# Scores in smaller matmul tiles, fewer evictions, paced transfers and new engine orders in the last stage of a five-stage transformer kernel

## The reference, cut to what matters

```
for i in range(6):
    x = attn_layer(shift_tokens(x), Wqkv[i], q_scale[i], k_scale[i], Wo[i]) + x
    x = ffn_layer(shift_tokens(x), ln_g[i], ln_b[i], W1[i], b1[i], W2[i], b2[i]) + x
# attn_layer: 16 heads of 64
q = l2norm(q) * qs;  k = l2norm(k) * ksc
q = q * cos * scale + rotate_half(q) * sin * scale        # rotate_half: (-x2, x1)
k = k * cos / scale + rotate_half(k) * sin / scale
# local_attention: windows of 32 queries, each sees its own and the last window: 64 keys
sim = einsum('bhwie,bhwje->bhwij', bq, bk2) * 8.0
sim = where((it < jb) | (it > jb + 32) | (jb == -1), -max, sim)
out = einsum('bhwij,bhwje->bhwie', softmax(sim), bv2)
```

## Time and profile before

| | us |
|---|---|
| median of 3 runs | 4817.93 (4815.92 to 4821.29) |
| span of the profiled execution, first to last instruction | 4799.2 |
| TensorE busy in it | 4554.0 |
| VectorE busy | 3761.7 |
| GpSimd busy | 3692.6 |
| ScalarE busy | 3501.1 |

### The profile page before, as it was taken

The page is one execution under the profiler, slowest core; times in us unless marked ns, Lnnn a source line. Parts: engine busy times, 40 slices in busy tenths (PEclk is TensorE's granted clock), DMA queues, the critical chain, the costliest instruction groups (busy, mean ns, idle before and its releaser), DMA issues.

```text
span 4799.2 us, 114895 instructions
## 1 busy us (share of the span) xinstructions
PE 4554.0 (95%) x44512; PEld 3128.6 (65%) x44512; DVE 3761.7 (78%) x5226; ACT 3501.1 (73%) x6738; POOL 3692.6 (77%) x2336
## 2 busy tenths in 40 slices
PE   7998999987887799999999999999999999999997
PEld 5666768874443466666666666666666666666665
DVE  6776556658999688888888888888888888888885
ACT  3454756557775688888888888888888888888885
POOL 2222334438998999999999999999999999999993
PEclk9898999998999999999999999999999999999998
DMA  2000000004332222232222322232322322322222
GB/s 79 1 2 1 2 1 1 1 1 168 150 142 106 55 63 63 56 85 70 54 67 65 75 68 55 68 75 61 68 64 67 76 53 66 80 64 63 62 56 52
DMA packets 164292, 289.06 MB, mean 60 GB/s; under 512 B 44063, under 2 KB 61351, under 8 KB 159655
## 3 DMA queue, kind: packets, MB, share of 16 engines
q1 hardware_dynamic: 162310, 281.46, 22.3%
q10 hardware_dynamic: 1440, 0.24, 0.0%
HBM read 90.22 MB, written 2.62 MB: 19 GB/s over the span
## 4 chain that ended last, share of the span: by engine, by line
PE 59%; ACT 3%; issue 2%; DVE 1%; POOL 1%; ACTq 0%; DVEq 0%; POOLq 0%
PE ps L2559 18%; PE ps L2614 8%; PE ps L2588 8%; PE ps L2572 7%; PE ps L2627 7%; PE ps L2601 3%; PE ps L2669 3%; PE ps L2660 3%; PE ps L2653 3%; ACT L3f_pT L2820 2%; PE ps L2634 1%; PE ps L2640 1%; ACT L3f_kT L2803 1%; POOL L3f_t L3155 0%; POOL L3f_raw L3172 0%
## 5 line engine op out<-in xcount | busy, mean ns | idle before, releaser
L3155 POOL TENSOR_TENSOR L3f_t<-L3f_raw,L3f_rot 128x512 f32<-128x512 f32 x768 | 1007.7, 1334 | 268.3 <-DVE L3f_raw L2971 268.3
L2559 PE MATMUL ps<-L3f_wqkv,all_z 128*128 128x512 f32 x2304 | 1133.7, 601 | 12.8 <-DVE L3f_raw L2971 11.7
L3172 POOL TENSOR_TENSOR L3f_raw<-L3f_raw,L3f_t 128x1024 f32<-128x1024 f32 x384 | 961.4, 2504 | 3.8
L3164 POOL TENSOR_TENSOR L3f_raw<-L3f_raw,L3f_rot 128x1024 f32<-128x1024 f32 x384 | 953.8, 2484 | 3.8
L2971 DVE TENSOR_TENSOR L3f_raw<-ps,L3f_ri 128x512 f32<-128x512 f32 x768 | 495.6, 682 | 231.9 <-ACT L3f_ri L2778 230.2
L2954 DVE TENSOR_REDUCE L3f_ss<-L3f_sqr 128x8 f32<-128x512 f32 x768 | 507.8, 681 | 163.2 <-ACT L3f_sqr L2768 160.8
L2572 PEld LDWEIGHTS ps<-all_ident,L3f_raw 128*128 128x128 f32 x3072 | 358.7, 141 | 320.7 <-issue 282.8
L2559 PEld LDWEIGHTS ps<-L3f_wqkv,all_z 128*128 128x128 f32 x2304 | 385.2, 191 | 221.0 <-issue 151.5
L2572 PE MATMUL ps<-all_ident,L3f_raw 128*128 128x128 f32 x3072 | 472.3, 276 | 49.1 <-ACT L3f_kT L2803 27.1
L2820 ACT ACTIVATE L3f_pT<-ps 64x512 f32<-64x512 f32 x768 | 453.2, 590 | 83.9 <-PE ps L2601 75.9
L2768 ACT ACTIVATE L3f_sqr<-ps 128x512 f32<-128x512 f32 x768 | 449.9, 599 | 76.5 <-PE ps L2559 71.7
(11 more groups left out here) (333 smaller groups left out, 8702.0 us busy)
## 6 DMA issues: line engine op xcount, KB each, us to landing
L3f_vw<-L3f_v SPq DMA_DIRECT2D x1344, 128.0 KB, 2.4
L3a_Bs<-L3a_rows SPq DMA_DIRECT2D x16, 2048.0 KB, 7.1
L3a_Cs<-L3a_rows SPq DMA_DIRECT2D x16, 2048.0 KB, 11.6
L3f_vw<-L3f_v SPq DMA_DIRECT2D x192, 64.0 KB, 2.1
L3f_wqkv<-in_L_ffn_Wqkv SPq DMA_DIRECT2D x24, 256.0 KB, 2.9
L3f_wqkv<-in_L_ffn_Wqkv SPq DMA_DIRECT2D x6, 512.0 KB, 3.6
L3f_wo<-in_L_ffn_Wo SPq DMA_DIRECT2D x48, 64.0 KB, 2.3
out<-all_x SPq DMA_DIRECT2D x8, 256.0 KB, 3.6
```

Of the source, the lines that this page charges most:

```text
L2559: p.matmul(PS[:, j % 3, :], Z[:, u % NSEQ, t * P:t * P + P], w, start=True, stop=True).then_inc(proj.sem)
L3155: op = g.tensor_tensor(t[:, :, to], r[:, :, fr], w[:, 1, to].unsqueeze(1).broadcast_to((P, H, WIN)), ALU.mult)
L3164: g.tensor_tensor(r, r, w[:, 0, :].unsqueeze(1).broadcast_to((P, H, HD)), ALU.mult).then_inc(cosined.sem)
L3172: g.tensor_tensor(r, r, t, ALU.add).then_inc(rotated.sem)
```

## The change

It touches the last stage alone.

- Scores: q is evicted as it comes, into `qT`, in one operation for each group of four pairs; no zeros. A score matmul takes the 64 rows of one head, 32 columns of weights (a window's queries) and 64 keys. Windows go to the four quarters of the PSUM partitions, heads of a pair to banks 6 and 7. There are 64 matmuls a call in place of 32.
- The mask has one row of keys for all windows. `below` writes `sm` with the two heads of a pair side by side.
- `spread` evicts two blocks of 64 x 1024 in place of four of 64 x 512; `pT` still has its zeros, and the value matmuls keep their number and shape.
- `sine` is one operation, whose read goes through the halves of a head backwards.
- The 16 transfers of a unit have two semaphores in turn, and each waits for the last but one.
- The four lists of calls are in another order, and the outer loop runs from -4 to N/2 + 2.

```
-        lmaskb = self.sb("lmaskb", [P, TILES, 2, KEYS], BF16)
+        lmaskb = self.sb("lmaskb", [P, TILES, KEYS], BF16)
-        qz = self.sb("qz", [P, TILES, PAIRS, NW, 2, WIN])
+        qT = self.sb("qT", [P, TILES, PAIRS, P])
-        sm = self.sb("sm", [P, TILES, H, KEYS])
+        sm = self.sb("sm", [P, TILES, PAIRS, 2, KEYS])
-        pT = self.sb("pT", [P, TILES, 2 * PAIRS, 2, 2, WIN])
+        pT = self.sb("pT", [P, TILES, PAIRS, NW, 2, WIN])
 # sp
-                for part, shift in ((WIN, 0), (0, 1)):
-                    for half in range(2):
-                        for w in range(NW):
-                            ...
-                            s.dma_start(to, v2[...]).then_inc(v_put[k % 2].sem, 16)
+                pieces = [(part, shift, half, w) for part, shift in ((WIN, 0), (0, 1)) for half in range(2) for w in range(NW)]
+                for n, (part, shift, half, w) in enumerate(pieces):
+                    landed = v_put[k % 2][n % 2]
+                    if n >= 2:
+                        s.wait_ge(*landed.at(k // 2, 16 * (n // 2) - 1))
+                    ...
+                    s.dma_start(to, v2[w * WIN:(w + 1) * WIN, k % 2, 0:e, half, :]).then_inc(landed.sem, 16)
 # scores
-                        r = slice(w % 2 * HD, w % 2 * HD + HD)
-                        mm = p.matmul(PS[r, 6 + w // 2, a * KEYS:(a + 1) * KEYS], qz[:, t, a, w, :, :].rearrange("p h q -> p (h q)"),
-                                      kT[:, a, t * P + w * WIN:t * P + w * WIN + KEYS], start=True, stop=True)
+                        for h, (r, _) in enumerate(halves):
+                            mm = p.matmul(PS[w * WIN:(w + 1) * WIN, 6 + h, a * KEYS:(a + 1) * KEYS], qT[r, t, a, w * WIN:(w + 1) * WIN],
+                                          kT[r, a, t * P + w * WIN:t * P + w * WIN + KEYS], start=True, stop=True)
 # turned
-                    for half in range(2):
-                        r = slice(half * HD, half * HD + HD)
-                        op = a.activation(qz[r, t, 4 * g:4 * g + 4, :, half, :], src[r, :, :].rearrange("p c (w q) -> p c w q", q=WIN), ACT.Copy)
+                    op = a.activation(qT[:, t, 4 * g:4 * g + 4, :], src, ACT.Copy)
 # spread
-                for r in range(2):
-                    for half in range(2):
-                        op = a.activation(pT[half * HD:(half + 1) * HD, t, r:2 * PAIRS:2, :, half, :], ..., ACT.Copy)
+                for h, (r, _) in enumerate(halves):
+                    op = a.activation(pT[r, t, :, :, h, :].rearrange("p a w q -> p (a w) q"), PS[r, 4:6, :].rearrange("p b (n q) -> p (b n) q", q=WIN), ACT.Copy)
 # below
-                v.tensor_tensor(sm[:, t, :, :], sc(), mx[:, t, :].unsqueeze(2).broadcast_to((P, H, KEYS)), ALU.subtract).then_inc(s_sub.sem)
+                v.tensor_tensor(sm[:, t, :, :, :].rearrange("p a h k -> p h a k"), sc().rearrange("p (h a) k -> p h a k", h=2),
+                                mx[:, t, :].rearrange("p (h a) -> p h a", h=2).unsqueeze(3).broadcast_to((P, 2, PAIRS, KEYS)), ALU.subtract).then_inc(s_sub.sem)
 # sine
-                for half in range(2):
-                    to, fr = slice(half * WIN, (half + 1) * WIN), slice((1 - half) * WIN, (2 - half) * WIN)
-                    op = g.tensor_tensor(t[:, :, to], r[:, :, fr], w[:, 1, to].unsqueeze(1).broadcast_to((P, H, WIN)), ALU.mult)
-                op.then_inc(sined.sem)
+                g.tensor_tensor(t.rearrange("p h (b e) -> p h b e", b=2), r.rearrange("p h (b e) -> p h b e", b=2)[:, :, ::-1, :],
+                                w[:, 1, :].rearrange("p (b e) -> p b e", b=2).unsqueeze(1).broadcast_to((P, H, 2, HD // 2)), ALU.mult).then_inc(sined.sem)
 # outer loop
-        for i in range(-2, N // 2 + 1):
+        for i in range(-4, N // 2 + 3):
```

More of the change, by code:

```diff
@@ L2608, in values @@
                 if t == 0:
[L2609 removed]
+                    for e in range(2):
+                        p.wait_ge(*v_put[u % 2][e].all(u // 2))
                 for c in range(PAIRS // 2):
                     for w in range(NW):
[L2612 to L2616 removed]
+                        for to, n in halves:
+                            a = 2 * c + n
+                            mm = p.matmul(PS[to, 4 + c // 2, (c % 2) * 2 * P + w * HD:(c % 2) * 2 * P + (w + 1) * HD], vw[:, u % 2, t * NW + w, a * HD:(a + 1) * HD],
+                                          pT[:, t, a, w, :, :].rearrange("p h q -> p (h q)"), start=True, stop=True)
                 mm.then_inc(o_mm.sem)
@@ L2785, in value @@
                 if u >= 2:
-                    a.wait_ge(*v_put[u % 2].all(u // 2 - 1))
+                    for e in range(2):
+                        a.wait_ge(*v_put[u % 2][e].all(u // 2 - 1))
                 a.activation(v2[:, u % 2, int(x[1]), "ab".index(x[2]), :], PS[:, j % 3, :], ACT.Copy).then_inc(v_out.sem)
@@ L2872, in gelu @@
                     a.preload_act_table_set(EXP_LN)
-            value(2 * i + 2, "v1a")
+            affine(2 * i - 2)
+            exponent(2 * i, 1)
+            length(2 * i + 2, "q0")
+            turned(2 * i + 1, 0, 1)
+            turned(2 * i + 1, 0, 2)
+            squared(2 * i + 2, "k0a")
+            centred(2 * i - 1)
+            turned(2 * i + 1, 0, 3)
+            squared(2 * i + 2, "k0b")
+            root(2 * i - 1)
+            turned(2 * i + 1, 1, 0)
+            length(2 * i + 2, "k0")
+            value(2 * i + 2, "v0a")
+            turned(2 * i + 1, 1, 1)
+            spread(2 * i, 0)
+            value(2 * i + 2, "v0b")
+            squared(2 * i + 2, "q1a")
+            squared(2 * i + 2, "q1b")
+            turned(2 * i + 1, 1, 2)
+            output(2 * i, 0)
+            length(2 * i + 2, "q1")
+            turned(2 * i + 1, 1, 3)
+            squared(2 * i + 2, "k1a")
+            spread(2 * i, 1)
+            exponent(2 * i + 1, 0)
+            squared(2 * i + 2, "k1b")
+            affine(2 * i - 1)
+            exponent(2 * i + 1, 1)
+            output(2 * i, 1)
             gelu(2 * i - 1, 0)
             gelu(2 * i - 1, 1)
+            length(2 * i + 2, "k1")
+            value(2 * i + 2, "v1a")
             gelu(2 * i - 1, 2)
@@ L3172, in add @@
                 g.tensor_tensor(r, r, t, ALU.add).then_inc(rotated.sem)
+            add(2 * i + 2, "q0")
+            cosine(2 * i + 2, "k0")
+            add(2 * i + 2, "k0")
+            sine(2 * i + 2, "q1")
             cosine(2 * i + 2, "q1")
```

182 lines of the change are left out of this document (71 added, 111 removed).

## The result

The changed kernel takes 4793.8 us (median), the one before 4813.7 on the same chips: a ratio of 0.9967 with a 95% interval of 0.9952 to 0.9982. Faster by 0.3%, 16 to 20 us; the forecast was 170 us. Nearly all of the expected gain is missing, and the profile after shows three places where it went.

The account below looks back on a forecast made before the run. TensorE was taken to bound the last stage: 65.94 - 3.72 = 62.2 us a period, -175 us over 47 periods, +5 for layer changes, so 4817.9 - 170 = 4648 us. This case's range was 4570 to 4710, the overall range 4560 to 4815.

Parts of the forecast that it names:

- What bounds the kernel: Last stage: TensorE, busy 65.28 of 65.94 us a period; time saved there counts until GpSimd's 60.02 us stands in the way.
- lie beside TensorE: VectorE's mask, subtraction, sum and scaling: claimed unchanged, hidden beside TensorE with 11 us a period to spare.
- If all eight run beside each other it is 16 rounds of 59 ns = 0.94 us: Score call: 128 records in eight overlapping tiles; with 0.13 us kept beyond the rounds, 1.07 to 1.09 us.
- rival 1: Score matmuls: TensorE takes small records no faster than 28 to 29.5 ns, 3.6 to 3.8 us a call; about 5160 us, chance 0.17.
- rival 2: Score matmuls: no more than four tiles, or rows and columns not together; call stays 1.9 us; 4785 to 4820 us, chance 0.11.
- columns over tiles: Score matmuls: cost follows moving columns divided by tiles running side by side; 128 columns in one tile take 108 ns.
- 0.93 us a call: Score calls: time the new tiles were to save on TensorE, 3.7 us a period of four calls.
- TensorE's pieces are the same but for the scores: TensorE's work in the new orders: only scores change, each instruction waits only for data or banks; busy 61.6 of 62.2 us.
- The orders. I count 0, between -1.5 and +1.5: New lists of calls in the last stage: no effect counted, range -1.5 us (waits vanish) to +1.5 us a period.
- rival 3: GpSimd's reversed read costs more or new orders hold up the normalised rows; period 64 to 65 us, 4755 us, chance 0.16.
- The transfers: The values' 16 transfers, two at a time: train of about 20 us instead of 10.3, hidden before the values' matmuls.
- +5 us: Layer changes: weights queued behind the slower transfers stall TensorE 0 to 3 us, taken as 1 us in each of 5.

Follow-up runs that it names:

- e9: Changed kernel with ScalarE's three gelu calls together and q and k evicted as bfloat16, 128 instructions a score call: 0.9659 of the kernel before.
- e7: Changed kernel with the gelus together, score matmuls multiplying only 32 of 64 keys (output wrong): one run, 4776 us.
- e1: Changed kernel with ScalarE's three gelu calls next to each other again, the length of k1 behind them: 0.9905 of the kernel before.
- e8: Changed kernel with the gelus together and the other order of score tiles, heads outside and windows inside: 0.9897 of the kernel before.
- e6: Kernel before with score matmuls cut into 128 x 32 tiles, 256 instructions a call in place of 128: 1.0094 of the kernel before.
- e10: Kernel before with the new lists of calls and outer loop alone, gelus together: 1.0013 of the kernel before.
- e4: Changed kernel with the values' transfers issued back to back, as before: 1.0001 of the kernel before.
- e11: Changed kernel with the gelus together and the values' transfers back to back: 0.9913 of the kernel before.
- e14: Kernel before, with its old large score tiles, and q and k as bfloat16: 0.9797 of the kernel before.
- e2: Score tiles of the change alone, with the old lists of calls, back-to-back transfers and two sine operations: 0.9948 of the kernel before.
- e12: Repeat of e1 (changed kernel, gelus together) on the chip of e9 and e11: 0.9911 of the kernel before.
- e13: As e9, with every score matmul issued twice into the same place, 256 instructions a call: 0.9876 of the kernel before.

## Why the prediction was wrong

- **What bounds the kernel**: right as far as it went. TensorE had 65.28 of 65.94 us and the shortest period did follow the score call. VectorE's operations "lie beside TensorE" did not hold: their busy time stayed (3758 for 3762 us), but the longest waits of TensorE after, beside the standstills, are for VectorE.
- **"If all eight run beside each other it is 16 rounds of 59 ns = 0.94 us"** is the step that failed first. The eight do overlap, so rivals 1 and 2 are out. But between "columns over tiles" and rival 1's 28 ns lies a pace that I had only from a burst of eight: records are taken at 7.7 ns (e9, 0.485 us for 63 steps) to 8.6 (e7) at best and at 9.9 with f32 and 64 columns. The term "0.93 us a call" measured 0.61, 1.3 us a period less. My sign for this, 128 records in over 1.5 us, was too coarse: they took 1.48. The mean over 127 starts is 9.9 ns. By that, the 25 ns between starts that the Trainium skill states (TensorE: Matmul & The Clock Gate, section "Wait — 56ns, not 53.3ns?") does not hold across tiles.
- **"TensorE's pieces are the same but for the scores"** left out what the pieces are made of. The number of instructions per call doubled, from 128 to 256, and I priced their multiplying but not their arrival. Its price is 1.2 to 1.3 us a period on the mean (after, e1, e8), 1.0 in e6, where only the scores' instructions changed; the pauses at the borders alone sum to 49 us in the stage's 48 periods after.
- **"The orders. I count 0, between -1.5 and +1.5"**: the value was wrong and the cause could be read in the diff. `length` between two `gelu` calls means table loads; the trace of before had them at two lines, only around the trio. They cost 0.7 to 0.8 us a period (e1, e10). No rival of mine had the loads; rival 3 came nearest, since it had the new orders hold up the normalised rows, which is the way that the delay takes (`length`, `norm`, residual, `centre`; lines above). Its sum of 4755 us missed as well.
- **ScalarE**: 48 us a period forecast; e9 has 47.8 in 62.5. **GpSimd**: the one sine was to save 1.4 us a period. Its line's total fell from 1007.7 to 999.5 us in the run, about 0.2 a period: the mean is 2603 ns, the median 2367. I read the difference as longer operations that meet VectorE's scaling more often, which no run isolates. The reversed read itself costs nothing: the shortest takes 2342 ns, the shortest `cosine` of that size 2340.
- **The transfers**: the train of 20 us and its cover held; no matmul of the values waits for a landing. Of the "+5 us" for the layer changes, TensorE's waits for the output weights make 2.3 us, in 3 waits. A layer change does cost more than before, but for another reason: in e9, where periods are alike, it is 1.7 us against 0.5, and at each of the five TensorE's `turn_qk` waits 1.5 us for the end of VectorE's `gated` (the bank they share). The same five waits stand in the changed kernel (below) and in e4 and e11, whose transfers are not paced. So the term was about the right size, 6 us in five changes, by luck.

```profile
PE ps L2575 <- DVE L3f_gg L3038: 7.4, 5, 1.5
PE ps L2630 <- DMA L3f_wo<-in_L_ffn_Wo: 2.3, 3, 1.1
```

- **The sum**: 62.2 forecast, +1.3 for the pace, +0.8 for the loads, +1.3 for the standstills make 65.6 of the measured 66.0. The last 0.4 us is not settled. e9, with the calls' cost gone, has 63.1, and there TensorE is busy 59.9 and GpSimd 59.5 of 62.5 us: the hand-over between engines, which I had counted at 0, is worth some us as soon as TensorE gets faster. In e9 it is VectorE that TensorE waits for, most of all `turn_p` for `normal` (line 3031), 62 us in 45 waits.
- **The rivals**: the measured 4794 us lies inside the 4785 to 4820 of rival 2, but by chance: its condition, no more than four tiles at once, is refuted by 9.9 ns a record.

## What to carry to other kernels

Count instructions, not only columns, before cutting matmuls into smaller tiles: once tiles run beside each other, the pace at which instructions are taken (here 8 to 10 ns a record) and the arrival of their blocks of 256 set the time, and a burst that uses up most of a block in about 1 us stands still now and then. Fewer passes over the same tiles can be worth more than more tiles (e14 against e2, 2.0% against 0.5%), at the price of rounding q and k. And when an order is rewritten, read off where the activation tables change: a logarithm and an exponential between two gelus cost three loads here. What a delay is worth is then read from who waits at its end: here not the third gelu but `centre`, three steps on.

## What the runs showed of the hardware that I had not expected

- Eight tiles of 64 x 32 overlap, rows and columns at once: 9.9 ns a record (f32, 64 columns), where two tiles gave 29.5.
- Periods that had been equal to 0.01 us but for layer changes spread by 3.8 us (e6) when a burst of 128 TensorE instructions became 256.
- TensorE's instructions arrive in packets of 16.4 KB, 256 to a packet. No border between two was crossed less than 1.1 us after the packet had landed, in 17 traces, and every long call's pause ends there (1.1 to 1.6 us behind the landing in after, e12 and e13).
- Logarithm and exponential, which shared one preloaded table while they stood together (before), took a load each when they stood between gelus.
- A bfloat16 score call in two tiles of 128 x 64 (e14) and one in eight tiles of 64 x 32 (e9) last the same, 0.50 and 0.49 us.
